# Softmax attentions of a four-layer block: projections as three fp32r products from split parts, in another order

## The chip, the cores and the metric

The program runs on one core of a Trainium2 chip. What counts is the device time of one execution in microseconds (us). A core has TensorE (PE, with its weight loads PEld), VectorE (DVE), ScalarE (ACT), GpSimd (POOL) and SyncE (SP), which here only issues DMAs; each runs its own instructions in order, and they meet at semaphores.

## The reference

Four layers, each a cross-attention and a feed-forward part with gates, on x of 2 x 512 tokens with 512 features. The attention of every layer reads the same context of 2 x 1024 rows.

```
x = x + tanh(g_xattn[n]) * Ln_xattn(layernorm(x), ctx)
x = x + tanh(g_ffn[n])   * Ln_ffn(layernorm(x))
```

L0's attention is linear. L1, L2 and L3 have softmax attentions with 16 heads of 32 features:

```
Q, K, V = query @ Wq.T + bq, ctx @ Wk.T + bk, ctx @ Wv.T + bv
scores  = einsum('bhsd,bhtd->bhst', Q, K) / sqrt(32)
out     = einsum('bhst,bhtd->bhsd', softmax(scores), V) @ Wo.T + bo
```

L1 has a key mask, a layernorm after its output and a scaled residual; L2 rounds its queries, its output and two of its weights to int8 steps; L3 is plain.

## The kernel before

One function, streamed_attention_block, does the attention of L1, L2 and L3. Its work is eight sets in a layer: four groups of four heads (f), two batches (b), b changing fastest. A set has 32 units: eight tiles of 128 keys times four heads. A unit is one scores matmul on PE (L1450), in L1 a clip on DVE (L1636), and one exponential on ACT (L1545). After each key tile the four heads' products with the values (L1463) follow on PE; POOL adds up the probabilities (L1590), seven adds of 2048 columns a set; PE turns that sum into row sums in the next set (L1480), DVE inverts it, POOL normalises.

The scores are exact products though fp32r matmuls round their operands: keys and queries are split into a high and a low fp32r part (kh, kl, qh, ql), and three copies of each go by DMA into k_stack and q_stack, so that one matmul over 96 rows gives high x high + low x high + high x low. ACT writes the high parts from PSUM (L1526), DVE the low ones (L1618), SP issues the 24 stack DMAs of a set (L1373). L2 and L3 also need each query's largest score: 32 row matmuls a set on PE (L1430), 32 row maxima on DVE (L1624), a join (L1631), a transpose on PE (turn, L1437), a split on ACT and DVE (L1519, L1601) and two DMAs that fold the result into q_stack as two more rows (L1380). This is done for the next set during the present one, and the next set's first scores wait for the fold.

The projections of set n + 2 run in set n, as chunks between the units (CHUNK_AT): two key items, two value items and a query item, each of four chunks, in two PSUM banks used in turn. All of them are fp32 matmuls from ctxT, 4 MB of fp32 context in SBUF, xT, and the weights of a head group, loaded two groups ahead. Before the first set, the same items of sets 0 and 1 are made in the order FIRST_ITEMS, the last five of them between the rows of set 0.

```python
                    if i in (0, QUERIES) and n:
                        for h in range(HG):
                            act.wait_ge(stacked[h], STACKS * n)
```

This is the wait in the high part (high): kh holds all 1024 keys of a set, and may be written anew when the stack DMAs of the set before have landed.

Of the kernel before, what the change touches and what calls it, by code (L numbers as in the profile page):

```python
# [20 lines left out]
P = 128  # L21
# [18 lines left out]
TOKEN, PICKED = D, D + 1  # L40

# [82 lines left out]
def norm_block(env, name, split=None, quantised=False, load_context=None, rows=None, early_loads=None, router=None):  # L124
# [10 lines left out]
    with ExitStack() as local:  # L135
# [8 lines left out]
        with nc.Block() as block:  # L144
            if load_context:
# [13 lines left out]
            def _(dve):  # L159
# [22 lines left out]

                for t in range(TILES):
                    if not quantised:
                        normalised(t).then_inc(xn_done, 1)
                    elif t % 2 == 0:
                        for u in (t, t + 1):
                            last = normalised(u)
                        link(last)
                        quantise_rows(nc, link, xn[:, t % 4:t % 4 + 2, :], xn[:, t % 4:t % 4 + 2, :], top, tmp)  # L190
                        dve.sem_inc(xn_done, 2)
                if split:
# [10 lines left out]
            def _(pe):  # L203
                for t in range(TILES):
                    pe.wait_ge(xn_done, t + 1)
                    if t >= 4:
                        pe.wait_ge(copied, t - 3)
# [13 lines left out]
            def _(act):  # L221
                if not taken:
                    act.wait_ge(var_done, TILES)
                nc.scalar.activation(sd[:], meanvar[:, :, 1], ACT.Sqrt, bias=env.eps_ln[:]).then_inc(sd_done, 1)
                for t in range(TILES):
# [1020 lines left out]
class GroupWeights:  # L1246


    def __init__(self, env, name, local):
        def sb(n, shape):  # L1250
            return local.enter_context(env.nc.sbuf_tensor(f"{name}_{n}", shape, F32))

        env.prefix = f"{name}_weights"
        self.loaded = [env.sem(f"w_loaded{s}") for s in range(2)]
        self.tiles = {n: sb(n, [P, 2, m]) for n, m in (("wk", DC * P), ("wq", DC * P), ("wv", DC * P),
                                                       ("bk", 1), ("bq", 1), ("bv", P))}

    def load(self, env, sp, f):
        s = f % 2
        for n in ("wk", "bk", "wq", "bq", "wv"):  # L1260
            sp.dma_start(self.tiles[n][:, s], env.io[n][f]).then_inc(self.loaded[s], 16)
        sp.dma_start(self.tiles["bv"][:, s], env.io["bv"][f].partition_broadcast(P)).then_inc(self.loaded[s], 16)


def streamed_attention_block(env, name, aT, weights, keep_mask=None, wo_dram=None, rows_of_output=()):

# [13 lines left out]
    KT, QT, HALVES_K = CTX // P, SEQ // P, CTX // HALF  # L1280
# [4 lines left out]
    ROWS = HG * QT * HALVES_K  # L1285
    KEYS, QUERIES, VALUES = (0, 1), 2, (3, 4)
    TURN, SUMS = 5, 6
    less_max_rows = keep_mask is None
    S_SLOTS, R_SLOTS, P_SLOTS, V_SLOTS = 3 if less_max_rows else 5, 2, 3, 3
    SUMMED = range(SETS - 1 if less_max_rows else SETS - 2, SETS)  # L1290
    EARLY = 5
    FOLD, FOLDS = 3 * HD, 2
    AHEAD = 2
    SUMS_AT, TURN_AT, COPY_AT = 7, 28, 3
    FIRST_ROW, LAST_ROW, PV_AT = 5, 26, 2
# [3 lines left out]
    SPLIT_AT = {max(u for u in CHUNK_AT if CHUNK_AT[u][0] == i) + 1: i for i in range(5)}  # L1299
    LOW_AT = {u + (i == QUERIES): i for u, i in SPLIT_AT.items()}  # L1300
    INVERT_AT = {SUMS_AT + 1 + part: part for part in range(4)}
    NORM_KT = (SUMS_AT + 6) // HG
    STACKS, FOLDED, LOADS = 16 * 6, 16 * FOLDS, 16 * 6

    def rows_at(u):
        if not less_max_rows or not FIRST_ROW <= u <= LAST_ROW:
            return range(0)
        span = LAST_ROW - FIRST_ROW + 1
        return range((u - FIRST_ROW) * ROWS // span, (u - FIRST_ROW + 1) * ROWS // span)

    FIRST_ITEMS = [(0, 0), (0, 1), (0, 2), (0, 3), (0, 4), (1, 3), (1, 4), (1, 0), (1, 1), (1, 2)]

    def bank_order():
        order = list(FIRST_ITEMS)
        if less_max_rows:
            order.append((0, TURN))
        for n in range(SETS):
            for u in range(UNITS):
                if u == (PV_AT if n - 1 in SUMMED else SUMS_AT) and n:
                    order.append((n - 1, SUMS))  # L1320
                if u in CHUNK_AT and CHUNK_AT[u][1] == 0 and n + AHEAD < SETS:
                    order.append((n + AHEAD, CHUNK_AT[u][0]))
                if less_max_rows and u == TURN_AT and n + 1 < SETS:
                    order.append((n + 1, TURN))
        return order + [(SETS - 1, SUMS)]

    place = {item: j for j, item in enumerate(bank_order())}
    highs = {item: j for j, item in enumerate(it for it in bank_order() if it[1] not in (*VALUES, SUMS))}
    w_loaded = weights.loaded
    stacked = [env.sem(f"stacked{h}") for h in range(HG)]  # L1330
    folded, ones_made, stack_ones, summed = env.sem("folded"), env.sem("ones_made"), env.sem("stack_ones"), env.sem("summed")
    product_done, product_free, high_done = env.sem("product_done"), env.sem("product_free"), env.sem("high_done")
    scores_done, exp_done, clipped, pv_done = env.sem("scores_done"), env.sem("exp_done"), env.sem("clipped"), env.sem("pv_done")
    rows_done, max_done, joined = env.sem("rows_done"), env.sem("max_done"), env.sem("joined")
    norm_done, added, taken, inverted = env.sem("norm_done"), env.sem("added"), env.sem("taken"), env.sem("inverted")
    with ExitStack() as local:
# [1111 lines left out]
```

## Time and profile before

| | |
|---|---|
| time, median of 3 runs | 3205.35 us (3204.42 to 3211.92) |
| the profiled execution, its span | 3207.5 us |
| PE busy | 2715.4 us, 85% |
| DVE busy | 1735.5 us, 54% |
| ACT busy | 1174.7 us, 37% |
| POOL busy | 936.3 us, 29% |
| mean granted clock of PE | 0.927 of full speed |

The profiled execution is 2.15 us longer than the median of the runs. The softmax attentions go from their first key chunk to their last score at 560 to 892 us (L1), 1564 to 1985 (L2) and 2300 to 2719 (L3). In the rows below a time is in us from the span's start unless it is marked ns; what ended the idle time ahead of an instruction stands in brackets behind it.

### The profile page before, as it was taken

How to read it: one execution, taken by the hardware profiler on the slowest of the kernel's cores; microseconds unless marked ns; L12 is line 12 of the kernel's file. 1: busy time of each engine (PE TensorE's matmuls, PEld its weight loads, DVE VectorE, ACT ScalarE, POOL GpSimd, SP SyncE). 2: the span in 40 equal slices, each digit the busy share in tenths (PEclk: the TensorE clock that was granted, in tenths of full speed). 3: DMA queues.
4: the chain of work that ended last, by engine and by line, in shares of the span. 5: the costliest groups of instructions: out<-in, count | busy, mean ns of one | idle time of the engine just before them, and what ended most of it. 6: DMA issues, size and time to landing. Idle time of an engine off the chain costs nothing. (4 is left out here: it accounts for less than half of the span.)

```text
span 3207.5 us, 35987 instructions
## 1 busy us (share of the span) xinstructions
PE 2715.4 (85%) x11415; PEld 1643.6 (51%) x11415; DVE 1735.5 (54%) x3207; ACT 1174.7 (37%) x2510; POOL 936.3 (29%) x408
## 2 busy tenths in 40 slices
PE   7998797999765499999689997658689998789898
PEld 3555586554233366665454543346455542477555
DVE  2444676477666899893655554512356553534322
ACT  0111222466625788781134444111134444212111
POOL 0000000388331010100047664033236665222122
PEclk9988899999987799999799998779899998899999
DMA  9220212432200100100331220263422211111822
GB/s 288 92 97 23 73 59 80 107 77 67 53 30 0 53 27 27 53 27 13 103 71 42 59 51 26 85 200 68 132 65 58 60 30 47 57 58 44 275 56 45
DMA packets 107035, 230.77 MB, mean 72 GB/s; under 512 B 24192, under 2 KB 28800, under 8 KB 105472
## 3 DMA queue, kind: packets, MB, share of 16 engines
q1 hardware_dynamic: 94016, 199.81, 21.0%
q0 software_dynamic: 12864, 29.06, 3.9%
q8 instruction: 78, 1.28, 0.2%
q14 instruction: 77, 0.63, 0.1%
HBM read 136.57 MB, written 39.00 MB: 55 GB/s over the span
## 5 line engine op out<-in xcount | busy, mean ns | idle before, releaser
L1590 POOL TENSOR_TENSOR L_attn_total<-L_attn_total,L_attn_probs 128x2048 f32<-128x2048 f32 x120 | 546.3, 4553 | 151.2 <-ACT L_attn_probs L1545 146.3
L1624 DVE TENSOR_REDUCE L_attn_row_max<-L_attn_rows_ps 128x1 f32<-128x512 f32 x512 | 335.7, 684 | 267.5 <-PE L_attn_rows_ps L1430 264.5
L1545 ACT ACTIVATE L_attn_probs<-L_attn_s_ps 128x512 f32<-128x512 f32 x512 | 292.2, 596 | 421.5 <-PE L_attn_s_ps L1450 417.7
L1450 PE MATMUL L_attn_s_ps<-L_attn_q_stack,L_attn_k_stack 98*128 98x512 f32 (+1 forms) x768 | 379.6, 531 | 39.6 <-DMA L_attn_q_stack<-L_attn_ml 34.1
L479 PE MATMUL L_ffn_hidden<-L_ffn_x_high,L_ffn_up_high 128*128 128x512 f32 x688 | 296.2, 430 | 100.5 <-DVE L_ffn_routes L395 53.3
L361 ACT ACTIVATE L_ffn_sums<-sims 128x128 f32<-128x128 f32 x1024 | 315.3, 389 | 46.9 <-DVE L_ffn_routes L381 26.3
L1590 POOL TENSOR_TENSOR L_attn_total<-L_attn_probs 128x2048 f32<-128x2048 f32 x20 | 91.0, 4550 | 798.7 <-ACT L_attn_probs L1545 798.7
L1450 PEld LDWEIGHTS L_attn_s_ps<-L_attn_q_stack,L_attn_k_stack 98*128 98x128 f32 (+1 forms) x768 | 142.5, 195 | 264.7 <-issue 127.3
L479 PE MATMUL L_ffn_hidden<-L_ffn_x_low,L_ffn_up_high 128*128 128x512 f32 x688 | 273.1, 397 | 0.0
L1463 PE MATMUL L_attn_o_ps<-L_attn_probs,L_attn_values 128*32 128x512 f32 x1536 | 212.9, 627 | 26.1 <-ACT L_attn_probs L1545 22.8
L500 PE MATMUL L_ffn_y<-L_ffn_down_in,L_ffn_h 128*128 128x512 f32 x512 | 230.8, 597 | 2.0 <-DVE L_ffn_h L607 2.0
L1430 PE MATMUL L_attn_rows_ps<-L_attn_k_stack,L_attn_q_stack 96*128 96x512 f32 x512 | 207.1, 439 | 29.0 <-DVE L_attn_row_max L1624 27.6
L1545 ACT ACTIVATE L_attn_probs<-L_attn_s_ps,keep_mask 128x512 f32<-128x512 f32 x256 | 186.6, 777 | 95.9 <-DVE L_attn_s_ps L1636 95.3
L1419 PEld LDWEIGHTS L_attn_product_ps<-L_attn_wv,L_attn_ctxT 128*128 128x128 f32 x1536 | 207.0, 200 | 11.0 <-issue 1.7
L1414 PE MATMUL L_attn_product_ps<-L_attn_ctxT,L_attn_wk 128*128 128x512 f32 x384 | 199.0, 612 | 14.3 <-DMA L_attn_ctxT<-in_ctxT 10.7
L479 PEld LDWEIGHTS L_ffn_hidden<-L_ffn_x_high,L_ffn_up_high 128*128 128x128 f32 x688 | 132.4, 192 | 151.0 <-issue 81.4
L1419 PE MATMUL L_attn_product_ps<-L_attn_wv,L_attn_ctxT 128*128 128x128 f32 x1536 | 207.6, 284 | 0.0
L1636 DVE TENSOR_SCALAR L_attn_s_ps<-L_attn_s_ps 128x512 f32<-128x512 f32 x256 | 166.4, 692 | 65.9 <-PE L_attn_s_ps L1450 64.6
L343 POOL TENSOR_TENSOR L_ffn_up_low<-L_ffn_up_in,L_ffn_up_high 128x512 fp32r<-128x512 f32 (+1 forms) x30 | 66.6, 2224 | 457.3 <-ACT L_ffn_up_high L337 457.3
L479 PE MATMUL L_ffn_hidden<-L_ffn_x_high,L_ffn_up_low 128*128 128x512 f32 x432 | 172.8, 400 | 0.0
L1430 PEld LDWEIGHTS L_attn_rows_ps<-L_attn_k_stack,L_attn_q_stack 96*128 96x128 f32 x512 | 97.8, 191 | 115.8 <-DVE L_attn_row_max L1624 83.3
L479 PEld LDWEIGHTS L_ffn_hidden<-L_ffn_x_low,L_ffn_up_high 128*128 128x128 f32 x688 | 132.7, 193 | 36.7 <-issue 11.0
(282 smaller groups left out, 4277.1 us busy)
## 6 DMA issues: line engine op xcount, KB each, us to landing
L_attn_k_stack<-L_attn_kh SPq DMA_DIRECT2D x192, 128.0 KB, 2.3
L_attn_ctxT<-in_ctxT SPq DMA_DIRECT2D x8, 2048.0 KB, 12.7
L_attn_abs_in<-in_L_ffn_w SPq DMA_DIRECT2D x12, 1024.0 KB, 9.8
L_attn_k_stack<-L_attn_kl SPq DMA_DIRECT2D x96, 128.0 KB, 2.4
L_attn_q_stack<-L_attn_qh SPq DMA_DIRECT2D x192, 64.0 KB, 2.0
L_ffn_x_slots<-L_attn_blank SPq DMA_DIRECT2D x46, 258.5 KB, 10.8
L_ffn_xg<-L_ffn_x_slots POOLq DMA_DIRECT2D x46, 258.5 KB, 4.9
L_ffn_up_all<-in_L_ffn_w SPq DMA_DIRECT2D x16, 704.0 KB, 14.1
```

The lines of the kernel that those rows point to most:

```text
L361: last = nc.scalar.activation(sums[:, h, a * NK:(a + 1) * NK], sims[:, t, h, KEY_ROWS:KEY_ROWS + NK], ACT.Identity, bias=sims[:, t, h, bas ...
L479: last = nc.tensor.matmul(hidden_ps[0:m, b, side, :], w[:, i, e0:e0 + m], x_parts[xp][:, i, h * HALF:(h + 1) * HALF], start=(q == 0), stop ...
L500: last = nc.tensor.matmul(y_ps[:, t % YB, :], h_parts[hp][0:m, s, c, t * P:(t + 1) * P], down_parts[wp][0:m, s, c, :], start=(q == 0), sto ...
L1414: last = nc.tensor.matmul(bank(n, i), w[:, s, c * P:(c + 1) * P], moving, start=(c == 0), stop=(c == DC - 1))
L1419: last = nc.tensor.matmul(bank(n, i)[:, c * P:(c + 1) * P], ctxT[:, d, at:at + P], wv[:, s, d * P:(d + 1) * P], start=(d == 0), stop=(d == ...
L1430: nc.tensor.matmul(rows_ps[:, r % R_SLOTS, :], q_stack[0:FOLD, n % 2, h, q * P:(q + 1) * P], k_stack[0:FOLD, n % 2, h, i * HALF:(i + 1) * ...
L1450: nc.tensor.matmul(s_ps[:, v % S_SLOTS, :], k_stack[0:depth, n % 2, h, kt * P:(kt + 1) * P], q_stack[0:depth, n % 2, h, :], start=True, st ...
L1463: last = nc.tensor.matmul(o_ps[HD * h:HD * (h + 1), :], values[:, n % V_SLOTS, kt, HD * h:HD * (h + 1)], probs[:, g % P_SLOTS, h, :], star ...
L1545: nc.scalar.activation(probs[:, g % P_SLOTS, h, :], s_ps[:, v % S_SLOTS, :], ACT.Exp, **kinds).then_inc(exp_done, 1)
L1590: nc.gpsimd.tensor_tensor(total[:], first, probs[:, g % P_SLOTS], ALU.add).then_inc(added, 1)
L1624: nc.vector.tensor_reduce(row_max[:, r // HALVES_K, r % HALVES_K:r % HALVES_K + 1], rows_ps[:, r % R_SLOTS, :], AX_X, ALU.max, negate=True ...
L1636: nc.vector.tensor_scalar(scores, scores, BOUND / SCALE, -BOUND / SCALE, ALU.min, ALU.max).then_inc(clipped, 1)
```

## The change

The projections are made of three fp32r products (TERMS: high x high, high x low, low x high) in place of one fp32 product. Their operands are split into parts:

- The context is split once, in L0: ACT copies sixteen pieces of 128 x 512 to fp32r, POOL subtracts, and ACT issues sixteen stores of 512 KB into a tensor in DRAM (ctx_parts). L1 to L3 load from it the parts of one batch, as two halves of 2 MB, and the second batch's during set 1. ctxT is gone from these layers.
- The normed x and the query weights are split in the norm blocks; key and value weights are split as they are needed, by ACT (high_split) and DVE (low_split), from a buffer that SP fills.
- Sets go batch by batch: b = n // 4, f = n % 4. All eight query items are made at a layer's start and kept in aT, where the heads' outputs also go; their stack parts are made from there two sets ahead (high_queries, low_queries at units 9 and 10).
- Value items now hold two head groups (256 columns): of each pair of sets, each makes half. kh and kl hold half a set's keys (512), and each half has its own twelve stack DMAs.
- The products of probabilities and values are done for two key tiles at a time, at units 2, 10, 18 and 26. There are four probability slots in place of three. Rows stand at units 1 to 25, all of the first key half first; the turn is at unit 27.

```diff
+TERMS = ((0, 0), (0, 1), (1, 0))
...
-    CHUNK_AT = {u: (item, c) for item, units in ((3, (0, 1, 3, 4)), (4, (8, 9, 10, 12)), (0, (13, 14, 15, 16)),
-                                                 (1, (17, 18, 20, 21)), (2, (22, 23, 24, 26)))
+    SUMS_AT, TURN_AT, COPY_AT, PV_AT, PV_EVERY = 7, 27, 5, 2, 8
+    QUERY_HIGH_AT, QUERY_LOW_AT = 9, 10
+    CHUNK_AT = {u: (item, c) for item, units in enumerate(((0, 1, 3, 4), (8, 9, 11, 12), (14, 15, 16, 17), (20, 21, 23, 24)))
...
+    FIRST = [("Q", 0, f) for f in range(FG)] + [("K", 0, 0), ("K", 0, 1), ("V", 0, 0), ("V", 0, 1)]
+    WITH_ROWS = [("V", 0, 2), ("V", 0, 3)] + [("Q", 1, f) for f in range(FG)]
+    LAST = [("K", 1, 0), ("K", 1, 1)]
...
-        kh, kl = sb("kh", [P, CTX], F32R), sb("kl", [P, CTX], F32R)
+        kh, kl = sb("kh", [P, HALF], F32R), sb("kl", [P, HALF], F32R)
...
+                def stack_queries(n):
+                    sp.wait_ge(query_low, n + 1)
...
+                def stack_keys(n, i):
+                    sp.wait_ge(product_free, place["K", n, i] + 1)
...
+                for n in range(SETS):
+                    guests = [SPLIT_AT[n, u] for u in (14, 20, 27) if (n, u) in SPLIT_AT]
+                    if n and n + 1 < SETS:
+                        stack_keys(n + 1, 1)
+                    if len(guests) > 1:
+                        load_raw(guests[0])
+                    if n + AHEAD < SETS:
+                        stack_queries(n + AHEAD)
+                    if len(guests) > 1:
+                        load_raw(guests[1])
+                    if n + AHEAD < SETS:
+                        stack_keys(n + AHEAD, 0)
+                    if guests:
+                        load_raw(guests[-1])
...
+                    elif kind == "K":
+                        _, n, i = item
+                        if c == 0:
+                            pe.wait_ge(parts.ctx_loaded[i], 16 * (n // FG + 1))
+                            pe.wait_ge(split_low, split_place["k", n] + 1)
+                        for w, x in TERMS:
+                            last = nc.tensor.matmul(to, wk[:, w, c * P:(c + 1) * P], ctx[:, i, x, c, :],
...
+                        for d in range(half * DC // 2, (half + 1) * DC // 2):
+                            for x, w in TERMS:
+                                last = nc.tensor.matmul(to[:, c // 2 * PAIR * P:(c // 2 + 1) * PAIR * P],
...
+                def high_keys(n, i):
+                    act.wait_ge(product_done, place["K", n, i] + 1)
+                    if n or i:
+                        for h in range(HG):
+                            act.wait_ge(stacked[h], STACK * (KH * n + i))
+                    nc.scalar.activation(kh[:], bank(("K", n, i)), ACT.Identity, bias=bk[:, n % FG:n % FG + 1]).then_inc(key_high, 1)
...
+                def low_split(w):
+                    to, of = split_of(w)
+                    dve.wait_ge(split_high, split_place[w] + 1)
+                    nc.vector.tensor_tensor(to[:, 1, :], of, to[:, 0, :].bitcast(F32), ALU.subtract).then_inc(split_low, 1)
...
+                def low_queries(n):
+                    dve.wait_ge(query_high, n + 1)
+                    nc.vector.tensor_tensor(ql[:], queries_of(n), qh[:].bitcast(F32), ALU.subtract).then_inc(query_low, 1)
...
+                for j in range(PIECES):
+                    if j % (PIECES // BATCH) == 0:
+                        act.wait_ge(ctx_loaded[j // (PIECES // BATCH)], 16)
+                    if j >= PART_SLOTS:
+                        act.wait_ge(part_stored[j % PART_SLOTS], 16 * (j // PART_SLOTS))
+                    nc.scalar.copy(part[:, j % PART_SLOTS, 0, :], context_piece(j)[0]).then_inc(part_high, 1)
+                    if j:
+                        store_part(j - 1)
```

## Rows read from the trace of the kernel before

**Rows 1.** Windows of steady sets of L3: busy us (instructions) of each engine, clock, DMA share.
```profile
2499.70:2548.30 48.60, 44.80 (x225) 24.60 (x225) 27.85 (x43) 20.65 (x37) 33.09 (x9) 1.00 0.22 50
2548.30:2598.60 50.30, 46.44 (x226) 25.55 (x226) 27.86 (x43) 20.65 (x37) 33.19 (x9) 0.97 0.21 48
```
**Rows 2.** Timeline of PE at a set's end in L3: start, us, instruction, [idle before].
```profile
2444.68 0.28 PE L1437 MATMUL L_attn_product_ps<-ident,L_attn_less_max 128*16 128x128 f32 x1
...
2449.50 0.50 PE L1450 MATMUL L_attn_s_ps<-L_attn_q_stack,L_attn_k_stack 98*128 98x512 f32 x1 [2.04 <-DMA L_attn_q_stack<-L_attn_ml]
```
**Rows 3.** Windows: a steady set of L1.
```profile
707.80:746.00 38.20, 35.96 (x194) 18.81 (x193) 27.23 (x42) 25.57 (x36) 33.09 (x9) 1.00 0.27 63
```
**Rows 4.** Timeline of POOL in L1, the first add of a set.
```profile
719.30 4.55 POOL L1590 TENSOR_TENSOR L_attn_total<-L_attn_probs 128x2048 f32<-128x2048 f32 x1 [3.17 <-ACT L_attn_probs L1545]
```
**Rows 5.** Timeline of PE at the start of L3's attention.
```profile
2299.97 9.10 PE L1414 MATMUL L_attn_product_ps<-L_attn_ctxT,L_attn_wk 128*128 128x512 f32 x16 [5.12 <-DMA L_attn_ctxT<-in_ctxT]
2308.91 3.60 PE L1414 MATMUL L_attn_product_ps<-L_attn_xT,L_attn_wq 128*128 128x512 f32 x8
2312.35 8.20 PE L1419 MATMUL L_attn_product_ps<-L_attn_wv,L_attn_ctxT 128*128 128x128 f32 x72
```
**Rows 6.** Timeline of PE in L0_ffn: fp32r matmuls of 512 columns, one after another.
```profile
371.89 0.39 PE L479 MATMUL L_ffn_hidden<-L_ffn_x_high,L_ffn_up_high 128*128 128x512 f32 x1
372.12 0.39 PE L479 MATMUL L_ffn_hidden<-L_ffn_x_low,L_ffn_up_high 128*128 128x512 f32 x1
```
**Rows 7.** Timeline of SP at the start of L3's attention: stack DMAs being issued.
```profile
2323.54 0.59 SPq L1373 DMA_DIRECT2D L_attn_k_stack<-L_attn_kl  x1
2324.18 0.59 SPq L1373 DMA_DIRECT2D L_attn_k_stack<-L_attn_kh  x1
```
**Rows 8.** The page's DMA issues: queue, count, KB each, median us from issue to landing.
```profile
L_attn_k_stack<-L_attn_kh SPq DMA_DIRECT2D x192, 128.0 KB, 2.3
...
L_ffn_x_slots<-L_attn_blank SPq DMA_DIRECT2D x46, 258.5 KB, 10.8
```
**Rows 9.** Timeline of POOL in L1_ffn: first and last of eight subtractions of 2048 elements.
```profile
998.20 4.51 POOL L343 TENSOR_TENSOR L_ffn_up_low<-L_ffn_up_in,L_ffn_up_high 128x2048 fp32r<-128x2048 f32 x1 [3.76 <-ACT L_ffn_up_high L337]
...
1410.88 4.57 POOL L343 TENSOR_TENSOR L_ffn_up_low<-L_ffn_up_in,L_ffn_up_high 128x2048 fp32r<-128x2048 f32 x1 [50.78 <-ACT L_ffn_up_high L337]
```
**Rows 10.** Timeline of DVE beside the first and last of those subtractions.
```profile
998.22 5.69 DVE L374 SCALAR_TENSOR_TENSOR L_ffn_sums<-L_ffn_sums,bar 128x512 f32<-128x512 f32 x2
...
1411.33 0.69 DVE L607 TENSOR_TENSOR L_ffn_h<-L_ffn_silu,L_ffn_hidden 128x512 f32<-128x512 f32 x1 [4.47 <-ACT L_ffn_silu L536]
1412.50 3.50 DVE L374 SCALAR_TENSOR_TENSOR L_ffn_routes<-L_ffn_sums,bar 128x512 f32<-128x512 f32 x1 [0.48 <-ACT L_ffn_sums L361]
```
**Rows 11.** Line L374 as a whole: ns min/median/max, first and last start.
```profile
L374 DVE SCALAR_TENSOR_TENSOR L_ffn_sums<-L_ffn_sums,bar x192: 735/745/5030, 998.2 to 1453.2; 128x512 f32<-128x512 f32 x192
```
**Rows 12.** Timeline of DVE at L3's start: first row maximum, last split.
```profile
2321.10 0.69 DVE L1624 TENSOR_REDUCE L_attn_row_max<-L_attn_rows_ps 128x1 f32<-128x512 f32 x1 [0.71 <-PE L_attn_rows_ps L1430]
...
2347.36 0.74 DVE L1618 SCALAR_TENSOR_TENSOR L_attn_ql<-L_attn_product_ps,L_attn_bq,L_attn_qh 128x512 fp32r<-128x512 f32 x1
```
**Rows 13.** Timeline of ACT at L3's start.
```profile
2348.90 1.28 ACT L1545 ACT_TABLE_LOAD   x1
2352.50 0.60 ACT L1545 ACTIVATE L_attn_probs<-L_attn_s_ps 128x512 f32<-128x512 f32 x1 [2.32 <-PE L_attn_s_ps L1450]
```
**Rows 14.** Timeline of L1's start: first key chunks and first exponential.
```profile
560.27 8.56 PE L1414 MATMUL L_attn_product_ps<-L_attn_ctxT,L_attn_wk 128*128 128x512 f32 x16 [5.61 <-DMA L_attn_ctxT<-in_ctxT]
...
599.37 0.78 ACT L1545 ACTIVATE L_attn_probs<-L_attn_s_ps,keep_mask 128x512 f32<-128x512 f32 x1
```
**Rows 15.** Waits of ACT from 560 to 610 (L1's start): us in total, times, longest.
```profile
ACT L_attn_kh L1526 <- DMA L_attn_q_stack<-L_attn_ql: 19.0, 1, 19.0
```
**Rows 16.** Timeline of ACT in L0: its first work after the norm's copies.
```profile
83.59 0.69 ACT L1884 ACTIVATE L_attn_kT<-L_attn_proj_ps,L_attn_bk 128x512 f32<-128x512 f32 x1 [60.60 <-PE L_attn_proj_ps L1829]
```
**Rows 17.** Windows: the same stretch of L0.
```profile
20.00:80.00 60.00, 57.53 (x147) 26.41 (x146) 13.80 (x25) 2.72 (x6) 0.00 (x0) 1.00 0.99 299
```

More of the change, by code:

```diff
@@ L121, in finish, with norm_block @@
         dve.wait_ge(self.var_done, TILES)
-def norm_block(env, name, split=None, quantised=False, load_context=None, rows=None, early_loads=None, router=None):
+def norm_block(env, name, split=None, quantised=False, load_context=None, rows=None, early_loads=None, router=None, queries=None):
     nc = env.nc
@@ L191, in _ @@
                         dve.sem_inc(xn_done, 2)
+                if queries:
+                    for t in range(TILES - 4, TILES):
+                        low_part(t)
+                    dve.wait_ge(low_done, TILES)
                 if split:
@@ L206, in _ @@
                     if t >= 4:
-                        pe.wait_ge(copied, t - 3)
+                        pe.wait_ge(low_done if queries else copied, t - 3)
                     for c in range(DC):
@@ L1243, in _ @@
                     first["vector_tile"](dve, t)
-class GroupWeights:
+class AttentionParts:
     def __init__(self, env, name, local):
[L1250 to L1262, printed above, removed]
@@ L1265, in streamed_attention_block, with sb @@
-def streamed_attention_block(env, name, aT, weights, keep_mask=None, wo_dram=None, rows_of_output=()):
+        def sb(n, shape, dt=F32):
+            return local.enter_context(env.nc.sbuf_tensor(f"{name}_{n}", shape, dt))
+        env.prefix = f"{name}_parts"
+        self.k_stack = sb("k_stack", [P, 2, DC, CTX], F32R)
+        self.total = sb("total", [P, DC, SEQ])
+        self.bk, self.bq, self.bv = sb("bk", [P, DC]), sb("bq", [P, DC]), sb("bv", [P, D])
+        halves = [self.k_stack[:, b].rearrange("p h (k c) -> p (h k) c", c=HALF) for b in range(BATCH)]
@@ L1311, in streamed_attention_block, with item_of, rows_at @@
-    FIRST_ITEMS = [(0, 0), (0, 1), (0, 2), (0, 3), (0, 4), (1, 3), (1, 4), (1, 0), (1, 1), (1, 2)]
+    STACK, FOLDED = 16 * 3, 16 * FOLDS
+    V_ITEMS = KT // 2
+    def item_of(n, number):
+        return ("V", n // 2 + 1, n % 2 * 2 + number) if number < 2 else ("K", n + AHEAD, number - 2)
+    def rows_at(n, u):
+        first = 1 if n else 5
+        if not less_max_rows or not first <= u <= LAST_ROW:
+            return range(0)
+        span = LAST_ROW - first + 1
+        return range((u - first) * ROWS // span, (u - first + 1) * ROWS // span)
@@ L1323, in bank_order @@
                 if less_max_rows and u == TURN_AT and n + 1 < SETS:
-                    order.append((n + 1, TURN))
-        return order + [(SETS - 1, SUMS)]
+                    order.append(("T", n + 1))
+        return order + [("S", SETS - 1)]
     place = {item: j for j, item in enumerate(bank_order())}
-    highs = {item: j for j, item in enumerate(it for it in bank_order() if it[1] not in (*VALUES, SUMS))}
-    w_loaded = weights.loaded
+    key_splits = {item: j for j, item in enumerate(it for it in place if it[0] == "K")}
@@ L1456, in pv @@
                     if kt == 0:
[L1457 removed]
+                        pe.wait_ge(product_free, place["V", n // PAIR, V_ITEMS - 1] + 1)
                         if n:
@@ L1528, in exponential, with high_turn @@
+                def high_turn(n):
+                    act.wait_ge(product_done, place["T", n] + 1)
+                    if n:
+                        act.wait_ge(folded, FOLDED * n)
+                    nc.scalar.copy(mh[:], bank(("T", n))[0:HG * QT, 0:P]).then_inc(turn_high, 1)
                 def exponential(n, u):
@@ new lines, in keep_values @@
+                def keep_values(pair, j):
+                    dve.wait_ge(product_done, place["V", pair, j] + 1)
+                    if pair >= V_SLOTS and j == 0:
+                        dve.wait_ge(pv_done, KT * PAIR * (pair - V_SLOTS + 1))
+                    of = pair % (FG // PAIR) * PAIR * P
+                    nc.vector.tensor_tensor(values[:, pair % V_SLOTS, 2 * j:2 * j + 2, :],
+                                            bank(("V", pair, j)).rearrange("p (t e) -> p t e", t=2),
+                                            bv[:, of:of + PAIR * P].unsqueeze(1).to_broadcast([P, 2, PAIR * P]),
+                                            ALU.add).then_inc(product_free, 1)
@@ L2415, in lay_out @@
             a[f"L{n}_attn_w{m}"] = up(i[f"L{n}_xattn_W{m}"], P)
-            a[f"L{n}_attn_b{m}"] = column(i[f"L{n}_xattn_b{m}"])
+            a[f"L{n}_attn_b{m}"] = (columns if n else column)(i[f"L{n}_xattn_b{m}"])
         for m in ("v", "o"):
```

554 lines of the change are left out of this document (359 added, 195 removed).

## The prediction

> **What bounds the kernel now.** On the page TensorE is the busiest engine by far, but that is a mean over stages, so I read the three softmax attentions set by set; nothing else is changed but the norms ahead of them and an idle stretch of L0. The windows of L3 (L2 has the same shape) show steady sets of 48.6 and 50.3 us, in which PE works 44.8 and 46.4, VectorE 27.9, ScalarE 20.7, GpSimd 33.1 [rows 1]. PE sets the pace there, except at a set's end, where the timeline shows a wait that ends last: the transpose of the row maxima (turn) starts at 2444.68, SyncE folds the result into the query stack by two DMAs, and the next set's first score starts at 2449.50, 4.82 us later, 2.04 of it plain waiting for the fold [rows 2]. The two lengths of set differ in the granted clock, 1.00 against 0.97: after that hole TensorE falls to half its 2.4 GHz for a few us in every other set, which costs 1.7. In L1 a set takes 38.2 with PE at 36.0 and POOL at 33.1 [rows 3]. POOL is all but a second bound there: its adds stand back to back but for one gap of 3.17 a set, in which the last add releases the sums on PE and the next probabilities are made [rows 4].
>
> **What the change takes from PE.** Next I read the pace of the matmuls from their starts. Four query chunks take 2308.91 to 2312.35, 0.86 us each, and nine value chunks 8.20, 0.91 each, eight 128-column instructions of 0.114 [rows 5]. An fp32r matmul of 512 columns starts 0.23 after the one before [rows 6], so a chunk of three terms is 0.69. A value chunk becomes six fp32r matmuls of 256 columns, which no row shows: at least 0.114 each (0.68 a chunk), at most 0.23 (1.38). I take half of 0.23 and a few ns, 0.119, so 0.71, as the 128-column instructions already load their weights at that pace. A steady set then loses 8 x 0.17 on keys, 4 x 0.86 on queries (all made ahead), 8 x 0.20 on values: 6.4 us. Making two key tiles' products with the probabilities in one visit moves work and removes none: nothing, with 0 to -1 a set open.
>
> **What it adds to a steady set of L2 and L3.** kh and kl now hold 512 keys, not 1024. The copy of the second key half (high_keys) waits until all twelve stack DMAs of the first have landed; queued behind it on ACT are the exponentials, behind its subtraction (low_keys) on DVE the join of the row maxima, and behind that PE's turn. In time: without waits the turn, at 43.8 in a 48.6 us set, would come at 37.4. The first half's chunks end after 18 of the 27 units before it, 24.9; copy 0.68, subtraction 0.75 and what is queued ahead of them, 27.1; twelve issues 0.63 apart [rows 7] put the last 7.0 later, and a 128 KB stack lands 2.3 after its issue [rows 8]: 36.4. Copy, subtraction, join, turn: 38.6. With the 4.82 behind the turn the period is 43.4. PE has little to do from 37 to 43, so I expect the half clock in every set: +1.8, 45.2 against a mean of 49.4. Six sets: -25 a layer (bounds: all hidden, 42.2 and -43; twice the clock's price, 47 and -15). Sets 6 and 7 lose no chunks, and the second batch's context is read again during set 1: it is wanted some 10 us after it lands, but its 2 MB delay the stacks beside it. Together -1 (-6 to +4).
>
> **Held by GpSimd.** The new DVE work has a property that the old in these sets has not: low_queries and low_split read two SBUF operands. L1_ffn shows what that costs. POOL subtracts 2048 elements from 1410.88 to 1415.45 [rows 9]; a DVE instruction on two SBUF operands starts beside it at 1412.50, takes 3.50 and ends 0.55 after POOL, while one that reads PSUM kept its 0.69 just before [rows 10]. The held line's median is 0.745, its longest 5.03 [rows 11]. The same happens at all eight POOL subtractions of that size, the first of them at 998.20. In the attentions row maxima, clips and kl read PSUM and so pass the adds. An L2 or L3 layer has six low_queries and four value-weight splits ahead of its rows (the other splits stand behind the turn or before the first add). POOL is busy 68% of a set; half a 4.57 add times 0.68 is 1.5, of which PE's lead of two row banks hides about 1. I take 0.5 each: +5 a layer (0 if they fall into POOL's gaps; 2.8 each, as in rows 10, +28). The Trainium skill (SBUF — State Buffer, SBUF: two separate sides) calls the port pair of these engines an exclusive lock, held for the whole instruction, between GpSimd and a DVE operation with two SBUF inputs; the trace agrees on DVE's side. By that rule alone each could wait a whole add of 4.55, +46 a layer.
>
> **Start of a layer.** Here the copy's wait costs more, since nothing runs beside it. Before, L3's PE starts at 2299.97 [rows 5], the 32 rows run from 2321.10 to 2347.36 [rows 12], and the exponentials' table load and first exponential start at 2348.90 and 2352.50 [rows 13]: 52.5 after PE. Changed, counted from PE's start: four query items at the cold clock to 12.5, two key items 15.2 and 17.9. Query stacks are issued from 8.6 to 16.3, key stacks of half 0 from 17.0, landing 26.3. Only then comes the copy of half 1 (27.1); its subtraction (27.9) frees the bank that the second value item wants, and PE has stood 7 us. Rows begin at 32.4; they took 26.3 with five other DVE operations between, now nine: 28.9, to 61.3. Turn 62.0. Only behind it stand the two key items of set 1: first half 64.8, split 66.5, twelve issues and landing 75.9, copy of the second half 76.7, and the first exponential is behind that on ACT; table load 1.28: 78.0. That is +25.5, less 3.5 for the three units of work that PE has done by then: +22 for L3 and for L2 (+11 if only one of the two round trips shows, +28 with nothing given back). L1 has no rows: its first exponential came 39.1 after PE's start [rows 14]. Now seven items of 2.75 from 28.0 end at 48.8, query stacks are issued to 55.4, key stacks land 65.2, first exponential 67.3: +28, less 2, +26. The wait itself is not new: ACT stood 19.0 us at L1's start until landed stacks let it write the next set's kh [rows 15]. It was one trip, and is two.
>
> **The rest.** L1's sets: PE falls to 29.6, but POOL's 33.1 and its gap of 3.17 allow 36.3, -8 over the steady sets (-12 to 0); holds between DVE and POOL add about 1.4 a set, +7: -1. The norms: eight DVE subtractions and the weight splits beside the transposes; the cover is the 5.1 that PE waited for the context [rows 5]. +1 each (-3 to +3). L0: sixteen copies, subtractions and 512 KB stores in the 60.6 us that ACT is idle until 83.59 [rows 16]. The DMA engines are at 0.99 there [rows 17], full of blank stores that land in 10.8 [rows 8]; with three slots sixteen stores take up to 16 x 10.8 / 3 = 58 us from about 22: 80. Just hidden: +1 (0 to +8, if ACT comes late to the key copies).
>
> **Sum** on the profiled span of 3207.5: L0 +1, norms +3, starts 26 + 22 + 22 = +70, sets of L2 and L3 2 x (-25 - 1) = -52, held DVE 2 x 5 = +10, L1's sets -1: +31, 3238.5. The runs' median, 3205.35, is 2.15 lower, so 3236.
>
> **Rivals.** (a) PE's saving comes out whole: the second copy finds its stacks landed, DVE is not held, the clock stays up, and only one round trip shows at the start. For it: PE is busy 92% of a set, and ACT, DVE and POOL have room. Against: the chain above is 1.2 longer than PE's own way, and nothing covers it at the start. It decides if the first half is split before 25.9 of a set, not 27.1. L2 and L3: sets -38 - 1, start +11, -28 each; L1: start +13, sets -4; with +4: -43, 3162 (3135 to 3188). (b) The holds are dear: ten at 2.8 in place of 0.5, +23 a layer: 3282. For it: eight of eight in L1_ffn. Against: DVE has 20 us of slack a set; it decides once a hold outlasts PE's lead of two banks. (By the whole-add rule of the skill's page it would be some 3318.) (c) The saving on values does not come: 256 columns cost as 512, +0.67 x 8 in twelve sets, +64: 3300. Against: the weight loads of the 128-column chunks keep up with 0.114.
>
> **How the numbers follow.** Forecast 0.57 (own range 3208 to 3264), (a) 0.25, (b) 0.13, (c) 0.05. For eight in ten the range goes down to 3155, into (a), and up to 3288, into (b). A difference under 0.3%, 9.6 us, can't be told from none. (a) is all but wholly faster: 0.25 in all; of the forecast about a fifth lies below 3215: same 0.13; slower 0.62.
>
> **What would show it.** Right: L3's first exponential 75 to 80 us after PE's start, ACT's kh copies waiting twice for k_stack DMAs there, a PE hole of 7 us near 20; steady sets of L2 and L3 at 44 to 47 with PE at 38 to 39, the second kh copy waiting for a stack DMA in each, the clock below 1 in all; L1's sets at 36 to 38; a maximum of low_queries well over 0.7. Wrong: starts as short as before (the order of waits is off, then a), sets under 42 or not under 48, value matmuls at 0.23, or ACT in L0 past 90.

## The result, and the profile after

The changed kernel takes 3319.45 us (median of 4 runs, 3311.65 to 3326.14) where the kernel before took 3204.89 beside it: ratio 1.0353, interval 1.0334 to 1.0371, 3.5% slower. The forecast was 3236 and its range ended at 3288; the direction was right, the size and the range were not. The profiled execution has a span of 3316.8, 109.3 more than before.

Where the 109 come in is read from the same marks in both traces, each with its lag behind the kernel before:

| mark | before | after | lag | gained since the mark above |
|---|---|---|---|---|
| L1, PE's first projection | 560.27 | 560.04 | -0.2 | -0.2 |
| L1, first exponential | 599.37 | 627.86 | 28.5 | +28.7 |
| L1, last exponential ends | 894.0 | 969.6 | 75.6 | +47.1 |
| L2, PE's first projection | 1564.1 | 1645.2 | 81.1 | +5.5 |
| L2, first exponential | 1617.85 | 1723.89 | 106.0 | +24.9 |
| L2, last exponential ends | 1985.4 | 2081.2 | 95.7 | -10.3 |
| L3, PE's first projection | 2299.97 | 2393.43 | 93.5 | -2.3 |
| L3, first exponential | 2352.50 | 2474.70 | 122.2 | +28.7 |
| L3, last exponential ends | 2719.4 | 2828.5 | 109.1 | -13.1 |

L0's new work is hidden. The starts cost 25 to 29 each. L2's and L3's sets give back 10 to 13, and L1's sets lose 47.

The start of L3 after, from three timelines: PE's, ACT's in two stretches.

```profile
2393.43 12.89 PE L1531 MATMUL L_attn_product_ps<-L_attn_k_stack,L_attn_wq_parts 128*128 128x512 f32 x48 [3.55 <-DVE L_attn_ones L1839]
2406.16 5.76 PE L1540 MATMUL L_attn_product_ps<-L_attn_ctx,L_attn_wk 128*128 128x512 f32 x24
2411.76 2.99 PE L1552 MATMUL L_attn_product_ps<-L_attn_wv,L_attn_ctx 128*128 128x256 f32 x24
2421.16 6.56 PE L1552 MATMUL L_attn_product_ps<-L_attn_wv,L_attn_ctx 128*128 128x256 f32 x30 [6.42 <-DVE L_attn_kl L1792]
```

```profile
2419.64 0.69 ACT L1682 ACTIVATE L_attn_kh<-L_attn_product_ps,L_attn_bk 128x512 fp32r<-128x512 f32 x1 [9.79 <-DMA L_attn_k_stack<-L_attn_kh]
```

```profile
2472.70 0.69 ACT L1682 ACTIVATE L_attn_kh<-L_attn_product_ps,L_attn_bk 128x512 fp32r<-128x512 f32 x1 [9.82 <-DMA L_attn_k_stack<-L_attn_kh]
2473.40 1.28 ACT L1707 ACT_TABLE_LOAD   x1
2474.70 2.14 ACT L1707 ACTIVATE L_attn_probs<-L_attn_s_ps 128x512 f32<-128x512 f32 x4
```

The order is the forecast's: four query items to 12.7 after PE's start, two key items to 18.3, PE's hole of 6.42 while ACT waits 9.79 for the stacks of the first key half, the second wait of 9.82 behind the rows, and the first exponential 81.3 after PE's start, where 52.5 stood in [rows 5, 13]. A value item of 24 matmuls takes 2.99, 0.72 a chunk: the 256-column price held too.

The sets, as windows of an odd set of L1, then of an odd and an even set of L3 (sets are counted from 0; columns as in [rows 1], which with [rows 3] they answer to):

```profile
754.90:801.80 46.90, 36.31 (x177) 20.83 (x177) 38.25 (x44) 26.58 (x40) 33.64 (x9) 0.83 0.27 68
...
2514.40:2567.00 52.60, 44.10 (x209) 26.06 (x209) 38.94 (x47) 22.14 (x40) 34.38 (x9) 0.87 0.35 101
2567.00:2611.90 44.90, 39.76 (x209) 24.94 (x209) 32.16 (x45) 21.08 (x38) 33.74 (x9) 0.92 0.38 106
```

The even set of L3 takes 44.9 where 45.2 was forecast, its clock below 1, and ACT's second kh copy in it waits 2.12 for a stack. The odd set takes 7.7 more; only the odd sets have splits of value weights. In L1 PE is busy no longer than before, but the set is 8.7 longer, the clock has fallen from 1.00 to 0.83, and DVE is busy 38.3 where it was 27.2. Most of DVE's extra busy time is not work but waiting. POOL, DVE and ACT at the start of that L1 set:

```profile
754.80 4.55 POOL L1768 TENSOR_TENSOR L_attn_total<-L_attn_total,L_attn_probs 128x2048 f32<-128x2048 f32 x1 [1.33 <-ACT L_attn_probs L1707]
```

```profile
755.26 4.64 DVE L1779 TENSOR_TENSOR L_attn_wk<-L_attn_raw,L_attn_wk 128x512 fp32r<-128x512 f32 x1 [0.82 <-ACT L_attn_wk L1668]
759.82 3.67 DVE L1825 TENSOR_SCALAR L_attn_s_ps<-L_attn_s_ps 128x512 f32<-128x512 f32 x6
```

```profile
760.54 4.12 ACT L1707 ACTIVATE L_attn_probs<-L_attn_s_ps,keep_mask 128x512 f32<-128x512 f32 x6 [4.63 <-DVE L_attn_s_ps L1825]
```

The add runs to 759.35; the weight split beside it ends 0.55 later, as in [rows 9, 10]. Six clips stand behind it, and ACT waits 4.63 for the first. Line L1779 as a whole (ns min/median/max) shows the same instruction with and without GpSimd at work:

```profile
L1779 DVE TENSOR_TENSOR L_attn_wk<-L_attn_raw,L_attn_wk x18: 692/4275/4645, 631.2 to 2706.4; 128x512 fp32r<-128x512 f32 x18
L1779 DVE TENSOR_TENSOR L_attn_wk<-L_attn_total,L_attn_wk x6: 681/687/693, 562.6 to 2421.0; 128x512 fp32r<-128x512 f32 x6
```

The six at a layer's start, where POOL has no adds, take 0.69; the eighteen inside the sets 4.28 at the median. In L3's odd sets the value splits are held too, and PE waits for the row maxima behind them (DVE, then PE):

```profile
2538.51 4.38 DVE L1779 TENSOR_TENSOR L_attn_wv<-L_attn_raw,L_attn_wv 128x512 fp32r<-128x512 f32 x1
...
2552.24 2.87 DVE L1779 TENSOR_TENSOR L_attn_wv<-L_attn_raw,L_attn_wv 128x512 fp32r<-128x512 f32 x1
```

```profile
2543.54 1.39 PE L1568 MATMUL L_attn_rows_ps<-L_attn_k_stack,L_attn_q_stack 96*128 96x512 f32 x2 [2.44 <-DVE L_attn_row_max L1813]
2555.85 0.47 PE L1568 MATMUL L_attn_rows_ps<-L_attn_k_stack,L_attn_q_stack 96*128 96x512 f32 x1 [2.63 <-DVE L_attn_row_max L1813]
```

### The profile page after: what moved, and what is told of

Same layout as the page of the kernel before. It is cut to its first block and busy times, and to the rows that moved or that the text cites. A ratio compares the mean times of both kernels' runs of the same rounds, so it can differ in the third digit from the quotient of the medians.

```text
span 3316.8 us, 36567 instructions
## 1 busy us (share of the span) xinstructions
PE 2702.4 (81%) x11319; PEld 1708.5 (52%) x11319; DVE 1898.5 (57%) x3303; ACT 1208.7 (36%) x2586; POOL 984.4 (30%) x438
## 5 line engine op out<-in xcount | busy, mean ns | idle before, releaser
L1768 POOL TENSOR_TENSOR L_attn_total<-L_attn_total,L_attn_probs 128x2048 f32<-128x2048 f32 x120 | 554.1, 4618 | 145.7 <-ACT L_attn_probs L1707 139.5
L1588 PE MATMUL L_attn_s_ps<-L_attn_q_stack,L_attn_k_stack 98*128 98x512 f32 (+1 forms) x768 | 334.7, 468 | 106.9 <-ACT L_attn_probs L1707 76.7
L1588 PEld LDWEIGHTS L_attn_s_ps<-L_attn_q_stack,L_attn_k_stack 98*128 98x128 f32 (+1 forms) x768 | 154.6, 208 | 262.6 <-ACT L_attn_probs L1707 119.1
L1568 PE MATMUL L_attn_rows_ps<-L_attn_k_stack,L_attn_q_stack 96*128 96x512 f32 x512 | 217.4, 448 | 45.3 <-DVE L_attn_row_max L1813 43.0
L1602 PE MATMUL L_attn_o_ps<-L_attn_probs,L_attn_values 128*32 128x512 f32 x1536 | 219.9, 687 | 9.6 <-ACT L_attn_probs L1707 9.4
L516 PEld LDWEIGHTS L_ffn_hidden<-L_ffn_x_high,L_ffn_up_high 128*128 128x128 f32 x688 | 132.6, 193 | 150.9 <-issue 81.1
L1552 PE MATMUL L_attn_product_ps<-L_attn_wv,L_attn_ctx 128*128 128x256 f32 x1152 | 188.7, 311 | 21.0 <-DVE L_attn_kl L1792 19.4
L1552 PEld LDWEIGHTS L_attn_product_ps<-L_attn_wv,L_attn_ctx 128*128 128x128 f32 x1152 | 187.3, 221 | 34.0 <-DVE L_attn_kl L1792 20.0
L155 POOL TENSOR_TENSOR L_attn_wq_parts<-L_attn_wq_raw,L_attn_wq_parts 128x512 fp32r<-128x512 f32 x12 | 15.4, 1311 | 632.6 <-ACT L_attn_wq_parts L259 632.6
L1540 PE MATMUL L_attn_product_ps<-L_attn_ctx,L_attn_wk 128*128 128x512 f32 x576 | 170.5, 419 | 15.2 <-DVEq L1837 15.2
```

The source lines that it names most:

```text
L516: last = nc.tensor.matmul(hidden_ps[0:m, b, side, :], w[:, i, e0:e0 + m], x_parts[xp][:, i, h * HALF:(h + 1) * HALF], start=(q == 0), stop ...
L1540: last = nc.tensor.matmul(to, wk[:, w, c * P:(c + 1) * P], ctx[:, i, x, c, :], start=(c == 0 and (w, x) == TERMS[0]), stop=(c == DC - 1 an ...
L1552: last = nc.tensor.matmul(to[:, c // 2 * PAIR * P:(c // 2 + 1) * PAIR * P], ctx[:, i, x, d, at:at + P], wv[:, w, d * PAIR * P:(d + 1) * PA ...
L1568: nc.tensor.matmul(rows_ps[:, r % R_SLOTS, :], q_stack[0:FOLD, n % Q_SLOTS, h, q * P:(q + 1) * P], k_stack[0:FOLD, n % 2, h, i * HALF:(i + ...
L1588: nc.tensor.matmul(s_ps[:, v % S_SLOTS, :], k_stack[0:depth, n % 2, h, kt * P:(kt + 1) * P], q_stack[0:depth, n % Q_SLOTS, h, :], start=Tr ...
L1602: last = nc.tensor.matmul(o_ps[HD * h:HD * (h + 1), :], values[:, n // PAIR % V_SLOTS, kt, at:at + HD], probs[:, g % P_SLOTS, h, :], start ...
```

## Experiments

Two theories stood after the trace. H: VectorE's subtractions of two SBUF operands wait out GpSimd's adds, with clips or row maxima behind them. K: the copy of the second key half waits for the stacks of the first. Each was taken away alone, then both. The kernel before measured 3204.9 beside the changed kernel and 3208.9 to 3211.1 beside the experiments, so ratios are compared; 1% is 32 us.

**GpSimd subtracts** (pool_lows). Inside the sets low_queries and low_split leave VectorE:

```diff
+                        if kt == 2 and n + AHEAD < SETS:
+                            pool_low_queries(n + AHEAD)
+                        for u in POOL_SPLIT_AT.get(kt, ()):
+                            if (n, u) in SPLIT_AT:
+                                pool_low_split(SPLIT_AT[n, u])
                         if kt and n not in SUMMED:
                             pool.wait_ge(exp_done, HG * (g + 1))
```

> Within the sets the second parts of queries and weights (low_queries, low_split) are subtracted by GpSimd between its adds, 1.3 us each, and no longer by VectorE; all else as in the changed kernel (3319). Theory H, that VectorE's two-operand subtractions wait out whole GpSimd adds and hold the clips of L1 and the row maxima of L2 and L3 behind them: L1's steady sets fall from 46 to about 41, L2's and L3's odd sets from 52 to 45, total 3319 - 30 - 2 x 14 = 3260. Theory K, that the copy of the second key half waiting for landed stacks sets the pace: sets stay within 1 us of what they were, total 3310 to 3325.

3267.17, ratio 1.0177 (1.0139 to 1.0215): 1.8% of the 3.5 are gone. Windows of an odd L1 set and of an even and an odd set of L3:

```profile
744.60:786.90 42.30, 34.26 (x177) 19.99 (x176) 25.86 (x41) 26.60 (x40) 38.05 (x12) 0.86 0.29 75
...
2520.60:2566.30 45.70, 40.49 (x209) 25.32 (x209) 27.20 (x42) 21.05 (x38) 34.63 (x10) 0.91 0.35 99
2566.30:2610.80 44.50, 39.90 (x209) 25.23 (x209) 27.21 (x42) 22.08 (x40) 38.32 (x13) 0.92 0.29 72
```

L3's odd set (here the one after the even set) is down from 51.8 to 44.5, L1's from 46.9 to 42.3, and DVE is back at 26 to 27 busy, while POOL now works 1.3 us for each subtraction. L3's even sets, from which a query split and a key split went, stay where they were: 45.7 and 44.4 for 44.9 and 45.3. From its first to its last exponential L1 is 25 us shorter, L2 17 and L3 14; the starts are within 2 us of what they were. Theory H holds; it is not all.

**A buffer for each key half** (two_halves), which three probability slots in place of four make room for:

```diff
-        kh, kl = sb("kh", [P, HALF], F32R), sb("kl", [P, HALF], F32R)
+        kh, kl = sb("kh", [P, KH, HALF], F32R), sb("kl", [P, KH, HALF], F32R)
...
-                    if n or i:
+                    if n:
                         for h in range(HG):
-                            act.wait_ge(stacked[h], STACK * (KH * n + i))
+                            act.wait_ge(stacked[i][h], STACK * n)
```

> kh and kl get a buffer for each key half, each with its own semaphores, so that the copy of the second half waits only for the stacks of the set before; three probability slots in place of four make room. Theory K: the starts lose both round trips, 7 and 9 us, first exponential from 81 to 65 us after PE's start in L3 and from 68 to 52 in L1; steady sets lose 2 us in L2 and L3, 4 in L1; total 3319 - 48 - 20 - 24 = 3230. Theory H: the starts fall as said, as nothing holds VectorE there, but sets stay; total about 3270. If three slots cost anything it shows as longer waits of exponentials for the adds.

3241.4, ratio 1.0099 (1.0065 to 1.0133): 2.5% gone. ACT at L3's start, which was PE's first projection at 2340.47:

```profile
2403.33 0.69 ACT L1683 ACTIVATE L_attn_kh<-L_attn_product_ps,L_attn_bk 128x512 fp32r<-128x512 f32 x1 [2.11 <-PE L_attn_product_ps L1540]
2404.04 1.28 ACT L1708 ACT_TABLE_LOAD   x1
2405.33 2.06 ACT L1708 ACTIVATE L_attn_probs<-L_attn_s_ps 128x512 f32<-128x512 f32 x4
```

The copy waits for PE and no longer for a DMA; the first exponential comes after 64.9 in place of 81.3 (L1: 48.7 in place of 67.8). An even and an odd set of L3:

```profile
2495.00:2538.00 43.00, 39.07 (x210) 24.80 (x210) 32.09 (x45) 20.93 (x38) 33.76 (x9) 0.94 0.39 112
2443.60:2495.00 51.40, 42.30 (x209) 26.37 (x209) 39.37 (x47) 22.06 (x40) 34.40 (x9) 0.90 0.35 103
```

The even one falls from 44.9 to 43.0, the odd one only from 52.6 to 51.4. The starts get 50 us shorter in all. But the sets gain too: from first to last exponential L1 and L2 are 12 us shorter, L3 8. So K sets the starts and has a part in the sets; what is left in the odd sets of L3 is H's.

**Both** (both).

> The two edits before together: GpSimd subtracts, and kh and kl have a buffer for each half (three probability slots). Theory H and K both at work: 3319 - 58 - 70 = 3190, L1's sets at 37 to 39, L2's and L3's at 42 to 44. If one of them hides behind the other the sum is less than the two singles by the overlap, some 10 to 30 us. If the changed order itself (pairs of key tiles, rows first half first) is at fault, L1's sets stay over 42.

3197.42, ratio 0.996 (0.9943 to 0.9976): 3.9% gone, which puts it 0.4% under the kernel before. The singles give 1.8 and 2.5, so they overlap by 0.4% only. L3's steady sets are at 42.5 to 45.4. L1's are still at 38.9 to 45.0, where 37 to 39 was expected. POOL's first add of two sets of L1 in a row:

```profile
738.82 4.71 POOL L1785 TENSOR_TENSOR L_attn_total<-L_attn_probs 128x2048 f32<-128x2048 f32 x1 [4.34 <-ACT L_attn_probs L1708]
...
781.46 4.69 POOL L1785 TENSOR_TENSOR L_attn_total<-L_attn_probs 128x2048 f32<-128x2048 f32 x1 [4.34 <-ACT L_attn_probs L1708]
```

Between the two POOL works without a gap until the 4.34 at the end: 38.3 us, 5.1 of them the four subtractions that were moved to it. So GpSimd sets the pace of L1's sets here: the edit that ends the holds puts their work on an engine that was all but a bound in L1 already.

**Keys of set 1 among the rows** (three):

```diff
+    WITH_ROWS = [("V", 0, 2), ("V", 0, 3)] + [("Q", 1, f) for f in range(FG)] + LAST
```

> As both, and the two key items of set 1 are made among the rows of set 0 and not behind the turn. What stands behind the turn at the start is then the fold alone: first exponential of L3 58 to 60 us after PE's start where both has 64, of L1 unchanged (no rows); so some 5 us less in L2 and L3 each than both. If VectorE paces the rows the two further splits cost 1.5 us there and the gain is 3 to 4 each.

3194.88, ratio 0.9955 (0.9937 to 0.9973). L3's first exponential comes after 61.7, 3.5 earlier than in both. The total is not to be told from that of both.

**What one held instruction costs** (before_two_operands, before_one_operand). Into the kernel before goes one instruction whose result nobody uses:

```diff
+                        if u in (12, 28) and n + AHEAD < SETS:
...
+                            nc.vector.tensor_tensor(spare[:], env.xT[:, 0, 0:SEQ], env.xT[:, 1, 0:SEQ], ALU.subtract).then_inc(spare_done, 1)
```

In the control the same place holds `tensor_reduce(spare[:, 0:1], env.xT[:, 0, 0:SEQ], AX_X, ALU.max)`.

> The kernel before, with one idle subtraction more on VectorE at units 12 and 28 of sets 0 to 5 of each softmax layer: 512 columns, both operands in SBUF (xT), result unused; 36 in all, 0.69 us each by themselves. Theory H, that such an instruction waits out the GpSimd add beside it: their mean is 2 to 3.5 us with a maximum over 4, L1's sets grow from 38.2 to 42 or more (two holds on the clip path), L2's and L3's by 1 to 3; total 3205 + 24 + 2 x 10 = 3250 (3230 to 3270). Rival: what costs is only that VectorE has more to do; then 36 x 0.6 at most, 3205 to 3225, as in the run with one operand.

> The control to the run with two operands: the same 36 places, but the instruction is a reduction over one SBUF operand of 512 columns, 0.68 us by itself. Theory H: it passes the adds, mean under 0.8, total 3205 to 3215. Rival: as slow as the run with two operands.

With two operands 3336.31, ratio 1.0387 (1.0362 to 1.0412); with one 3217.37, 1.0028 (1.0011 to 1.0045). The line of the added instruction, and a window of a steady set of L3, first with two operands, then with one:

```profile
L1677 DVE TENSOR_TENSOR L_attn_spare<-L_attn_xT x36: 895/3758/4359, 610.1 to 2758.7; 128x512 f32<-128x512 f32 x36
...
2534.70:2591.90 57.20, 48.00 (x225) 26.53 (x225) 34.01 (x45) 20.66 (x37) 33.31 (x9) 0.92 0.25 57
```

```profile
L1677 DVE TENSOR_REDUCE L_attn_spare<-L_attn_xT x36: 674/676/677, 610.5 to 2652.6; 128x1 f32<-128x512 f32 x36
...
2503.40:2554.20 50.80, 46.39 (x225) 25.89 (x225) 28.86 (x45) 20.66 (x37) 33.06 (x8) 0.97 0.21 47
```

Thirty-six instructions of 0.7 us cost 3.9% or 124 us; the expected 3250 was too low by 86. Over the control they cost 119 us, 3.3 each. The control differs in the second SBUF operand, but also in the operation and in what it writes. The subtractions of kl in the run with two operands settle that: like those of ql they write 512 columns too, but read one of their operands from PSUM. None of the 72 is held (0.752 at most), though 42 of them begin and end within a single GpSimd instruction. The line of kl:

```profile
L1619 DVE SCALAR_TENSOR_TENSOR L_attn_kl<-L_attn_product_ps,L_attn_bk,L_attn_kh x48: 739/750/752, 566.7 to 2748.9; 128x512 fp32r<-128x512 f32 x48
```

It is L2 and L3 that pay: their steady sets take 56.5 to 58.0, the control's 49.3 to 50.9; L1's mostly 41.2 against 38.2.

VectorE is idle 23 of the 57 us in the set shown, and its idle time hides nothing, because of where the instruction stands. The one at unit 12 has row maxima behind it. The one at unit 28 stands between the turn and the split that the fold waits for (DVE twice, then PE):

```profile
2585.35 3.88 DVE L1677 TENSOR_TENSOR L_attn_spare<-L_attn_xT 128x512 f32<-128x512 f32 x1
2589.16 0.27 DVE L1602 TENSOR_TENSOR L_attn_ml<-L_attn_product_ps,L_attn_mh 16x128 fp32r<-16x128 f32 x1
```

```profile
2591.91 0.79 PE L1451 MATMUL L_attn_s_ps<-L_attn_q_stack,L_attn_k_stack 98*128 98x512 f32 x1 [5.87 <-DMA L_attn_q_stack<-L_attn_ml]
```

PE waits 5.87 for the fold, 2.65 in the control and 2.04 in [rows 2]. So this prices a hold on the path; one that stands off it can be free, as the key split of 4.27 in the even sets of the changed kernel's L3, which are no shorter without it (pool_lows).

**Only the queries** (pool_queries): pool_lows without the weight splits.

> Only the queries' second parts (low_queries) go to GpSimd; the weight splits stay on VectorE. In the changed kernel's trace low_queries takes 0.97 in most sets of L2 and L3 and 2.8 in L1, the weight splits 4.3. If the holds cost what they last, six queries give back about 2 us each in L1 and nothing in L2 and L3: 3319 - 12 = 3307, and the weight splits are the other 40 of the 52 that moving both gave. Rival: the queries set the pace, as the stacks of the next keys stand behind them in SyncE's queue: 3280 or less.

3306.77, ratio 1.0306 (1.0273 to 1.0339): 0.5% of the 1.8. From first to last exponential it is 9 us in L1 and 3 each in L2 and L3. The weight splits are the larger part by far.

**Three probability slots alone** (p3): `P_SLOTS` 3 in the changed kernel, to see what two_halves paid for its room.

> The changed kernel with three probability slots in place of four and nothing else: the price of what the buffers for each key half had to give up. If the fourth slot is worth nothing: 3312 to 3326. If it lets GpSimd's adds lag in L1: L1's sets 1 to 3 us longer, 3325 to 3338; then the buffers for the halves alone are worth that much more than the 78 measured with three slots.

3318.48, ratio 1.034 (1.0307 to 1.0374): nothing. The fourth slot is worth nothing as long as the holds and waits are there.

**Each key tile's products at once** (three_single): three, with pv after each tile as in the kernel before.

```diff
-                        if u % PV_EVERY == PV_AT:
-                            g = KT * n + u // HG - 2
-                            for kt in range(max(g, 0), g + 2):
-                                pv(kt)
+                        if u % HG == PV_AT and KT * n + u // HG:
+                            pv(KT * n + u // HG - 1)
```

> The third corrected version (GpSimd subtracts, a buffer for each key half, keys among the rows), with the products of probabilities and values after each key tile again and not for two at a time. I costed the pairs at nothing. If that holds: 3190 to 3200 as without this edit. If the pairs bunch the probabilities' release and starve GpSimd's adds in L1 (gaps of 4.3 us there where the kernel before has 3.2): L1's sets 1 to 3 us shorter, total 3175 to 3188. If the pairs save PE switching: 1 us a set more, total 3210 to 3220.

3192.13, ratio 0.994 (0.9921 to 0.996), as without the edit. From first to last score, in the one trace of each, L2 is 4 us shorter, L3 1, L1 8 longer. The pairs, which were costed at nothing, may help L1 and cost L2 a little; in the total nothing shows.

**L1 as before** (mixed, mixed_single): L1 goes back to fp32 projections and its old order, L2 and L3 stay as in three or in three_single.

```diff
+                if masked:
...
+                    weights = GroupWeights(env, name, local)
+                    norm_block(env, name, load_context=lambda sp, group: weights.load(env, sp, group))
...
+                    whole_attention_block(env, name, heads_out, weights, keep_mask, env.io["wo"], early)
```

> L1 as in the kernel before (fp32 projections, its own loads and order), L2 and L3 as in the third corrected version, context parts still made in L0. Theory: L1's loss is all in its own block, 362 us from first matmul to last value product against 334, so 28 less: 3167. If L1's old form costs L2 or L3 something (loads, clock) it is 3170 to 3180.

> As mixed (L1 as before, L2 and L3 corrected), with the products of the probabilities after each key tile in L2 and L3. From the third version with single tiles, whose L2 took 329 from first to last score where pairs took 333, and L3 333 against 334: 3 to 8 us less than mixed, 3159 to 3164. If the difference there was chance: 3165 to 3170.

3166.71, ratio 0.9851 (0.9827 to 0.9876), and 3158.0, ratio 0.9836 (0.9804 to 0.9868). All of what was left in L1 was in its own block. The last is the fastest version of the study, 1.6% under the kernel before; the two can't be told apart.

## Why the prediction was wrong

In the marks of the table the working had +79 for the starts, -49 for the sets of L2 and L3 with their holds, -3 for L1's sets, and +4 for L0 and the norms. The trace has +82, -23, +47 and +3. Two of its steps failed: the price of a hold, and the sets of L1.

**The starts** were right: two round trips in the place of one, 81.3 for 78.0 in L3, 67.8 for 67.3 in L1, the hole of PE at its place, and two_halves takes them away. The 9 that the working took off for the units that PE has done by then fall to the sets in the table.

**The even sets of L2 and L3** were right: 44.9 for 45.2, with the stack wait of 2.1 and the fallen clock, and PE's saving at the price that was worked out. The odd ones, at 51.8 to 52.7, were not told apart from them.

**Held by GpSimd** is the first step that failed, in its price. That the new instructions would be held was read from [rows 9 to 11], and it came as read. But each of ten was put at 0.5: a hold of 1.5, of which PE's lead would hide 1. For the six low_queries that was about right: they last 0.68 to 0.97 in L2 and L3, and pool_queries gave 3 a layer. The four value splits last 2.85 to 4.39. PE's lead of two banks hid nothing that showed: in the odd set above the two splits last 7.25, PE waits 2.44 and 2.63 behind them, and the set is 7.7 longer than the even one. Taking all holds away (pool_lows) gave 17 and 14 in L2 and L3 from first to last exponential, where 5 each was summed. The mean over a random moment (half an add, times POOL's share) was also wrong for the key weights of L1, whose split does not come at random: the exponential of unit 27 releases an add and the copy behind it the subtraction, which so starts when the add has just begun (0.46 after it in the rows above).

**L1's sets**, put at -1, lost 47, the largest miss and the second step that failed. Two things of the text's own were not carried over to L1. The copy that waits for stacks stands in front of ACT's exponentials there too, and was priced for L2 and L3 alone. ACT's waits for it over the whole of L1 (us in total, times, longest):

```profile
ACT L_attn_kh L1682 <- DMA L_attn_k_stack<-L_attn_kh: 38.4, 6, 13.3
```

Two of the six, 23.1 together, belong to the start; 15.3 are the sets'. And the weight splits, which in L2 and L3 in part stand harmlessly behind the turn, have no turn to stand behind in L1: all of them are on the path of the clips, up to 4.64 each, where the working had 1.4 a set for all holds. pool_lows and two_halves show each alone, 24 and 31 from PE's first projection to the last exponential (19 of the 31 in the start, so 12 in the sets); both together give 28 in the sets. What the other 19 are is seen, for the steady sets, in the rows of POOL under "Both": there GpSimd, with the moved subtractions, sets the pace. The working had GpSimd allow 36.3, from its 33.1 and one gap of 3.17; in the trace of before, three gaps more, of 0.37 to 0.81, stand in each steady set of L1, 1.6 together.

**The range** ended at 3288 as rival (b) was priced for L2 and L3 alone. The page of the Trainium skill cited there (SBUF — State Buffer, SBUF: two separate sides) gave 3318 by holds of a whole add, close to what came, but by another way. In the table's marks that sum has +33 for the sets of L2 and L3 and -3 for L1's, where the trace has -23 and +47; that the totals meet is luck. The control experiment agrees with its rule, an exclusive lock for the whole instruction: 0.68 with one SBUF operand, 3.76 at the median with two.

**The norms** were put at +1 each. L2's cost 5.5: it has the quantised norm, in which DVE is the bound, so eight subtractions of 0.65 come on top, and GpSimd's weight subtractions hold some of its scalings (rows in the last section). L3's gave 2 back.

What the corrected versions still lose in L1, 28 us, is 9 in the start, which is longer with all queries made ahead, and 19 in the sets. Why GpSimd's one gap there is 4.34 and no longer 3.17, and what the half clock adds, no run separates.

## What to carry to other kernels

Before moving arithmetic to an engine with idle time, look what else its operands lock: an instruction on two SBUF operands on VectorE, beside a GpSimd that runs long adds, is priced at the add, not at itself, and what is queued behind it decides what that costs. The cure has a price too: the subtractions, moved to GpSimd, set the pace of L1. A buffer that is halved turns one wait into two; ask at each place where it is refilled, in each layer's own order, who stands behind the wait. Two small corrections, another engine for the subtractions and 4 KB more of buffer in each partition, were worth 3.9% or 126 us, more than the PE time that the change takes from all 18 steady sets (6.4 each, 115).

## What the runs showed of the hardware

Beside GpSimd adds of 4.55 us, 512 columns of subtraction from two SBUF operands take up to 4.64 where they take 0.69 alone; a reduction over one SBUF operand took 0.677 at most in 36 of 36, and subtractions with one operand in PSUM 0.752 at most in 72. GpSimd loses little by it: its adds take 4.62 in the mean in the changed kernel where they took 4.55.

One operand is not always safe. In L2's norm two scalings of 512 columns, each of one SBUF tensor by a scalar for each partition, took 2.81 beside two of GpSimd's weight subtractions and 0.88 without (DVE twice, then POOL):

```profile
1622.58 0.88 DVE L2246 TENSOR_SCALAR L_attn_norm_tmp<-L_attn_xn,L_attn_norm_top 128x512 f32<-128x512 f32 x2
...
1628.54 2.81 DVE L2246 TENSOR_SCALAR L_attn_norm_tmp<-L_attn_xn,L_attn_norm_top 128x512 f32<-128x512 f32 x2
```

```profile
1628.40 2.66 POOL L155 TENSOR_TENSOR L_attn_wq_parts<-L_attn_wq_raw,L_attn_wq_parts 128x512 fp32r<-128x512 f32 x2 [137.75 <-ACT L_attn_wq_parts L259]
```
